# Where TensorE transposes finished state products into y: behind both phases of a later slot's w, or between them

## The reference

```python
x = x + ssm(layernorm(x))
x = x + moe(layernorm(x))

def ssm(x):                                  # x: (B, T, D) = (2, 2048, 256), N = 16
    B_t, C_t = x @ W_B.T, x @ W_C.T          # (B, T, N)
    dt = softplus((x @ W_dt1.T) @ W_dt2.T + b_dt2)
    A = -exp(log_A)                          # (D, N)
    A_bar = exp(dt[..., None] * A)
    B_bar = (A_bar - 1) / (A + 1e-8) * x[..., None] * B_t[:, :, None, :]
    h_t = A_bar_t * h_(t-1) + B_bar_t        # a recurrence along T for each feature and state
    y_t = sum over n of h_t[:, :, n] * C_t[:, n]
    return y + D_skip * x

def moe(x):                                  # E = 8 experts, H = 1024
    e = argmax(softmax(x @ Wr + br))
    return gelu(x @ W1[e] + b1[e]) @ W2[e] + b2[e]
```

## Time and profile before

| | |
|---|---|
| time, median of 3 runs | 768.57 us (765.58 to 771.55) |
| profiled execution, its own time | 768.72 us |
| its span, first to last instruction | 766.9 us |
| mean granted TensorE clock | 0.963 of full speed |
| instructions | 17255 |

### The profile page before, as it was taken

One profiled execution on the slowest core, in us unless ns is written; L12 is line 12 of the kernel. 1 busy time (PEld: TensorE's weight loads), 2 busy tenths in 40 slices (PEclk: granted clock), 3 DMA queues, 4 the chain that ended last, 5 costly groups with the idle time before them and its releaser, 6 DMA issues. The chain is left out here.

```text
span 766.9 us, 17255 instructions
## 1 busy us (share of the span) xinstructions
PE 684.2 (89%) x5766; PEld 574.4 (75%) x5767; DVE 534.6 (70%) x907; ACT 470.6 (61%) x983; POOL 486.9 (63%) x609
## 2 busy tenths in 40 slices
PE   7798899998999988998878876769999999999993
PEld 6677777777777767776767775659899999977672
DVE  6879989999999899899899964335433433444440
ACT  3778998998989978879865764212222323325340
POOL 1799988979789878899986765333333433434321
PEclk9699999999999998999999987989999999999997
DMA  9577743243423521632825466221112111110100
GB/s 303 175 241 261 261 165 107 85 139 99 157 71 97 163 98 53 136 117 75 135 61 90 152 191 250 28 41 43 51 53 62 45 55 56 46 38 30 40 21 14
DMA packets 43999, 82.59 MB, mean 108 GB/s; under 512 B 5896, under 2 KB 14349, under 8 KB 43920
## 3 DMA queue, kind: packets, MB, share of 16 engines
q1 hardware_dynamic: 38288, 68.97, 29.9%
q0 software_dynamic: 5632, 12.61, 6.2%
HBM read 69.62 MB, written 13.52 MB: 108 GB/s over the span
## 5 line engine op out<-in xcount | busy, mean ns | idle before, releaser
L641 POOL TENSOR_TENSOR w_sb<-w_sb,Csb 128x512 f32<-128x512 f32 x202 | 255.0, 1274 | 54.1 <-DVE w_sb L1260 46.4
L1018 PE MATMUL WW<-b_sb,xin 64*128 64x130 f32 (+2 forms) x2304 | 203.8, 294 | 32.4 <-DVE w_sb L1260 14.2
L1018 PEld LDWEIGHTS WW<-b_sb,xin 64*128 64x128 f32 x2304 | 169.8, 194 | 79.2 <-issue 33.2
L1260 DVE TENSOR_TENSOR_SCAN w_sb<-WW,hlast,w_sb 128x512 f32<-128x512 f32 x152 | 187.4, 1268 | 4.0 <-PE WW L1018 2.2
L815 ACT ACTIVATE w_sb<-dt,negA 128x512 f32<-128x512 f32 x256 | 169.6, 709 | 9.1 <-DVE w_sb L1260 5.8
L891 ACT ACTIVATE dt<-WW,b1c 128x128 f32<-128x128 f32 x256 | 73.0, 388 | 155.2 <-PE WW L1135 137.6
L1056 PE MATMUL YY<-sm,w_sb 128*128 128x128 f32 x1024 | 142.6, 285 | 6.0 <-DVE row L1317 6.0
L709 POOL DMA_INDIRECT y_out<-CbX,ocol x36 | 43.3, 1203 | 150.5 <-DVE CbX L1639 144.6
L1056 PEld LDWEIGHTS YY<-sm,w_sb 128*128 128x128 f32 x1024 | 114.0, 144 | 20.8 <-POOL w_sb L641 5.0
L1172 PE MATMUL misc<-w_sb,dt 128*128 x512 | 119.1, 387 | 1.3 <-issue 0.8
L805 ACT ACTIVATE Csb<-w_sb,invA 128x512 f32<-128x512 f32 x136 | 93.3, 713 | 31.3 <-POOL w_sb L641 30.9
(11 more groups left out here) (267 smaller groups left out, 814.8 us busy)
## 6 DMA issues: line engine op xcount, KB each, us to landing
w_sb<-c_rows SPq DMA_DIRECT2D x86, 256.0 KB
CbX<-c_rows SPq DMA_DIRECT2D x42, 256.0 KB
w_sb<-w_in SPq DMA_DIRECT2D x20, 512.0 KB, 6.2
token_rows<-row SPq DMA_DIRECT2D x8, 1024.0 KB
w_sb<-w_in SPq DMA_DIRECT2D x24, 256.0 KB
xin<-x_in SPq DMA_DIRECT2D x8, 512.0 KB, 4.0
w_sb<-x_in SPq DMA_DIRECT2D x7, 512.0 KB, 8.4
b_sb<-b_in SPq DMA_DIRECT2D x1, 780.0 KB, 7.3
```

What stands on the lines that cost most here:

```text
L641: eng.tensor_tensor(hc[g % NHC], hb_of(g), Csb[i % NCS][:, :], ALU.mult).then_inc(s_hcp, 1)
L1018: return eng.matmul(to[:, a:a + width], x_rows[rows, k, h * P:(h + 1) * P], band[rows, k, at:at + width], start=start, stop=not start, ski ...
L1260: eng.tensor_tensor_scan(hb_of(g) if pooled(g) else w_of(g), w_of(g), A[g % NA], hlast[(q - 1) % 2][:, h * N + n:h * N + n + 1] if q % NC ...
```

## The change

In slots with n other than 1, `add_y` of the pair m - 2 is issued between the two phases of w of pair m + 2, and not behind both. The slot with n = 1 stays as it is (y ahead of both phases). No instruction is added or removed, no other engine's list is touched, and every wait stands at the instruction at which it stood.

```diff
                         add_y(KD * m - 4)
                         add_y(KD * m - 3)
                     make_w(m + 2, 0)
-                    make_w(m + 2, 1)
                     if n != 1:
                         add_y(KD * m - 4)
                         add_y(KD * m - 3)
+                    make_w(m + 2, 1)
```

## The result

Over four runs of each, the changed kernel takes 792.6 us (median) against 767.8 before: a ratio of 1.030 with a 95% interval of 1.022 to 1.038. The forecast was 785.5 us, with a range of 775 to 794: slower, by the mechanism foreseen, but 7 us short.

The account below looks back on a forecast made before the run. VectorE's scans set the scan stage's pace, TensorE close behind, so later w delays scans. Chunks 1 to 4 lose 9.6 us, then 2.0 + 2.0 + 1.7 + 1.5: 16.8 us on 768.7, forecast 785.5 us, range 775 to 794.

Parts of the forecast that it names:

- the step from phase 1 to a hop: TensorE's issue time from phase 1 to a 128-row hop, not in the trace before; taken as 0.65 us.
- The rival of cheap hops: Phase 1 to hop takes 0.45 us, so a chunk loses only 1.2 us: some 8 us, 777 us; chance 0.12.
- One chunk: Walk through chunk 3, repeated in chunks 1 to 4: lateness of w costs 2.4 us a chunk.
- Steps 1 to 3: Chunk 3, n = 2 to 10: delays add up until pair 60's scan and all from there are 1.54 us later.
- Step 5: n = 2 of a chunk: pair 50's w has slack 0.5 us, so its scan comes 0.4 us later.
- Step 4: n = 13: pair 63's w costs 0.89 us more, less 0.40 for VectorE's wait for a later hop, which goes.
- step 2: n = 4: the hop's earlier wait of 0.46 to 0.5 us for ScalarE absorbs delay, leaving it 0.41 us late.
- The other chunks: Outside chunks 1 to 4, losses of 2.0 us in chunk 0, 2.0 in 5, 1.7 in 6, 1.5 in 7.
- pair 127: Chunk 7, end of the stage: last w later by 0.89 us at full to 1.78 at half clock; taken 1.3.
- y's wait in chunks 6 and 7: GpSimd holds y, y phase 1, phase 1 the scan; up to 1.3 us in some six slots: 790 to 796; chance 0.09.
- Hidden: w's slack and ScalarE's and GpSimd's waits hide the delay: within 1%, some 769 to 774 us; chance 0.11.
- Faster by throughput: Shorter TensorE slots decide, not phase 1's lateness: near 1 us a chunk, 8 in all, 761 us; chance 0.04.

Follow-up runs that it names:

- x6: Changed kernel with only one unit's y (4 transposes) between the phases, the other's behind both, except at n = 1; 1.020 of the kernel before.
- x5: Changed kernel plus filler matmuls of zeros where TensorE stood idle (n = 2, 12 and 13, chunks 1 to 7); 1.018 of the kernel before.
- x2: Kernel before with the new order only in the slot n = 2 of each chunk; 1.006 of the kernel before.
- x4: Kernel before with the new order only in slots n = 3 to 11, all with hops; 1.012 of the kernel before.
- x7: Kernel before with the new order only in slots n = 0 and 15, which have no hops; 1.000 of the kernel before.
- x1: The changed kernel run again, unaltered, as second comparison with the kernel before; 790.8 us, ratio 1.036.
- x3: Changed kernel with the old order kept in the slots with n = 2; 1.018 of the kernel before.
- x8: Kernel before, old order, with y of slot n = 9 issued behind w of n = 10; 0.997 of the kernel before.
- x10: Changed kernel with filler matmuls of zeros (20) at n = 2 alone; 1.019 of the kernel before.
- x9: Kernel before, old order, with filler matmuls of zeros: 9 at n = 2, 6 ahead of the hop at n = 13; 0.997.

## Why the prediction was right, and by how much it was not

- **The sign and the mechanism** were right. The price of a slot, 0.89 us more from w's begin to w ready, is in the rows to a hundredth, and the choice of 0.65 for the step from phase 1 to a hop, between ends of 0.45 and 0.65, with it. The rival of cheap hops is out by that row. By the Trainium skill's rule on a change of the tiling mode ("TensorEngine Tiling (Array Packing)", Tiling Modes) the drain would be paid at each; the trace agrees with 0.2 us each time, and x6 shows that here the number of these changes does not set the loss.
- **One chunk** was forecast at 2.4 and takes 2.2 (x5, chunks 2 and 3). Steps 1 to 3, 1.54 by forecast, come in two parts: x2 has 0.3 for n = 2 and x4 1.0 for n = 3 to 11, 1.3 together. Step 5, 0.4 at pair 50, is kept with the whole change, as counted: in x5 pair 60's scan is 1.8 us late by the chunk's start (226.70 less 187.91, for 216.83 less 179.85). It is the 0.46 of slack at n = 4 that is spent once, by step 2 there and by step 5 in x7. Step 4: 0.88 for 0.89, against which 0.5 and not 0.4 is saved.
- **The other chunks.** x5's chunks 5 and 6 lost 0.6 and 0.8 us (55.5 for 54.9, both at a clock of 0.94, and 60.2 for 59.4, both at 1.00), where 2.0 and 1.7 were forecast: more of the lateness was hidden there than I had counted, behind which waits no run separates. At the end of the stage pair 127 waits 1.66 us at half clock and 0.89 at full, for 1.3.
- **The size** was short since the sum kept the clock of the trace before in every chunk but the last. I priced the wait at n = 2 as an order of events and not as idle time of TensorE. With the clock kept up by filler the whole costs 1.8%, 13.7 us, and 15.0 in the stage by the profile, somewhat under the forecast of 16.8. Without it the changed kernel costs 3.0 and 3.6%. The missing term is the clock, some 0.9 to 1.5 points or 7 to 11 us.
- **Luck.** The 792.6 us lie inside the range only because its upper part had been put there for another rival, y's wait in chunks 6 and 7, which is not seen. The range had nothing for the clock. The second comparison's loss, 26.7 us on 768.7, would be 795, just outside.
- **Rivals.** Hidden: refuted by 61 waits and 2.2 us a chunk. Faster by throughput: refuted by x1 and x5; in x7, where it should have shown alone, w at n = 0 waits for VectorE's scans and can't start earlier. y's wait becoming the bound in the late chunks: not seen, by chunk 6 above.

What stays open is when the clock falls. Much the same idle time at n = 2 (1.76 to 1.95 us) came with a fall in chunks 1 to 3 of x1 and with none in its chunk 4 or in chunks 1 to 4 of x2, and x3 fell behind 1.1 us late in chunks 1 and 2. Filling n = 2 keeps the clock up in chunks 1 to 4; what decides between these cases no run here shows. The size of the loss in any one execution stays open with it, some microseconds either way.

## What to carry to other kernels

Work moved into the gap of a two-phase producer saves the gap (0.13 us) and delays the product by the whole of what is moved (0.89 us). Where the consumer is the bound, that is a bad trade even if the producer is nearly as busy. So ask first which product is waited for last, and move work away from in front of that one (x8), not into it. And if a change makes TensorE wait longer in one piece, even once in 50 us, leave room for the clock beside the price of the wait; whether it falls, one longer wait alone does not tell (x2).

## What the runs showed of the hardware

- Idle times of 1.1 to 1.95 us on an otherwise busy TensorE were followed by 3.4 to over 9 us at half clock in some chunks (x1, chunks 1 to 3; x3, chunks 1 and 2) and not in others (x1, chunk 4; x2, chunks 1 to 4). 20 bf16 matmuls of zeros, 1.1 us of weight loads, at n = 2 of each chunk went with full clock in chunks 1 to 4 (x5, x10). The changed kernel was 1.2 to 1.8 points faster with them, the kernel before, with fewer of them, 0.3 (x9).
- A change from matmuls on 128 rows to ones on 64 or 32, or from 64 to 128, adds 0.2 us to the issue: 1.02 against 0.83 behind a transpose, 0.65 against 0.45 behind a matmul on 64 rows; 1.02 and 0.65 are the same in both orders.
